# Graph network on one core: node tiles below 52 split in row form and turned by DMA in the node update

## The reference, cut to what matters

```python
u = mish(jnp.concatenate([x, agg], axis=-1) @ W3 + b3)
out = u @ W4 + b4
y = x + out
mu = jnp.mean(y, axis=-1, keepdims=True)
var = jnp.mean(jnp.square(y - mu), axis=-1, keepdims=True)
return (y - mu) * jax.lax.rsqrt(var + LN_EPS) * gamma + beta
...
x = x + _L2_gnn_ref(h, ...)
h = jnp.maximum(_layernorm(x, axis=-1), 0.0)
x = x + _L3_gnn_ref(h, ...)
```

## Time and profile before

| | us |
|---|---|
| median of 3 runs | 2869.98 (2865.81 to 2870.67) |
| the profiled execution's own time | 2869.94 |
| its span, first to last instruction | 2867.5 |
| node update, first W3 matmul to its last VectorE instruction | 1900.3 to 2448.8 |
| PE busy over the span | 2449.1 (85%) |
| DVE busy | 1900.3 (66%) |
| ACT busy | 1508.1 (53%) |
| POOL busy | 1197.0 (42%) |

### The profile page before, as it was taken

One profiled execution on the slowest core, in us unless ns is written; L12 is line 12 of the kernel. 1 busy time (PEld: TensorE's weight loads), 2 busy tenths in 40 slices (PEclk: granted clock), 3 DMA queues, 4 the chain that ended last, 5 costly groups with the idle time before them and its releaser, 6 DMA issues. The chain is left out here.

```text
span 2867.5 us, 45056 instructions
## 1 busy us (share of the span) xinstructions
PE 2449.1 (85%) x13348; PEld 1420.4 (50%) x13348; DVE 1900.3 (66%) x4585; ACT 1508.1 (53%) x2234; POOL 1197.0 (42%) x1984
## 2 busy tenths in 40 slices
PE   0437998799879999899996988989999998899965
PEld 0424554344444445444553546766666665344443
DVE  7634887678657876799874445658888888323344
ACT  5524675445334543355434775658888777232261
POOL 5656775336333332355554531114444444001146
PEclk9998999999999999999998999999999999999975
DMA  8443453278757888766654332223333344101268
GB/s 200 166 154 111 149 151 104 101 189 203 140 116 186 208 179 153 204 221 221 202 183 141 103 105 74 83 94 126 117 124 117 132 148 136 57 1 42 60 233 343
DMA packets 379310, 414.16 MB, mean 144 GB/s; under 512 B 198240, under 2 KB 237573, under 8 KB 376206
## 3 DMA queue, kind: packets, MB, share of 16 engines
q1 hardware_dynamic: 350510, 337.43, 40.1%
q0 software_dynamic: 28640, 74.78, 9.0%
HBM read 172.55 MB, written 198.32 MB: 129 GB/s over the span
## 5 line engine op out<-in xcount | busy, mean ns | idle before, releaser
L218 PE MATMUL s_ps_z<-s_w,slots 128*128 128x512 f16 x2844 | 640.0, 383 | 7.9 <-DMA s_w<-split_self 7.9
L218 PEld LDWEIGHTS s_ps_z<-s_w,slots 128*128 128x128 f16 (+1 forms) x2844 | 279.5, 99 | 325.2 <-issue 10.7
L1649 ACT ACTIVATE s_g<-s_g,s_rn 128x512 f32<-128x512 f32 x237 | 169.8, 716 | 226.8 <-POOL s_rn L1508 226.7
L1508 POOL TENSOR_TENSOR s_rn<-s_em,minus_half 128x1 f32<-128x1 f32 x237 | 178.6, 754 | 219.6 <-DVE s_em L1577 214.5
L1558 DVE SCALAR_TENSOR_TENSOR s_g<-s_ps_z,s_f,s_bias 128x512 f32<-128x512 f32 x237 | 177.9, 751 | 109.6 <-PE s_ps_z L218 96.4
L2459 PE MATMUL u_ps_z<-slots,weights 128*128 (+2 forms) x1920 | 215.2, 273 | 4.1 <-PEq L166 4.1
L2595 PE MATMUL z_ps_z<-slots,weights 128*128 128x512 f16 (+1 forms) x960 | 211.8, 381 | 3.0 <-PEq L166 3.0
L2459 PEld LDWEIGHTS u_ps_z<-slots,weights 128*128 128x128 f16 x1920 | 186.4, 98 | 26.3 <-issue 4.3
L2564 DVE BATCH_NORM_STATS2 z_stats<-slots 128x6 f32<-128x512 f32 (+1 forms) x76 | 52.2, 687 | 187.2 <-ACT slots L2581 187.2
L1568 DVE SCALAR_TENSOR_TENSOR s_junk<-s_g 128x512 f32<-128x512 f32 x237 | 164.5, 694 | 4.1
L218 PE MATMUL s_ps_z<-s_wn,s_aT 128*128 128x512 f16 x720 | 165.2, 380 | 1.8 <-DVE s_aT L1392 1.8
(11 more groups left out here) (395 smaller groups left out, 5615.0 us busy)
## 6 DMA issues: line engine op xcount, KB each, us to landing
h_rows<-s_g SPq DMA_DIRECT2D x237, 256.0 KB, 2.4
x_rows<-q_x SPq DMA_DIRECT2D x79, 256.0 KB, 2.3
s_halves<-x_rows SPq DMA_DIRECT2D x79, 256.0 KB, 2.9
x_rows<-s_halves SPq DMA_DIRECT2D x79, 256.0 KB, 2.1
u_x<-x_rows SPq DMA_DIRECT2D x79, 256.0 KB, 2.9
x_rows<-u_x SPq DMA_DIRECT2D x79, 256.0 KB, 2.1
h_rows<-u_h SPq DMA_DIRECT2D x79, 256.0 KB
weights<-x_rows SPq DMA_DIRECT2D x79, 256.0 KB, 6.6
```

The lines of the kernel that those rows point to most:

```text
L218: ins = nc.tensor.matmul(out_ap, a(c), w[:, part * size + c * n:part * size + (c + 1) * n], start=first and c == 0 and m == 0, stop=stop a ...
L1508: nc.gpsimd.tensor_tensor(out=self.rn[b][:, :], in0=self.em[b][:, :], in1=minus_half[:, :], op=POW).then_inc(self.s_rn, 1)
L1649: nc.scalar.activation(self.g[b][:, :], self.g[b][:, :], ACT.Relu, scale=self.rn[v.buf(2)][:, 0:1]).then_inc(self.s_h, 1)
```

## The change

For tiles 0 to 51 (`PE_TURNS = 52`; steps 2 to 27 handle them) TensorE no longer transposes. ScalarE's `hi` reads the rows `u_h` and writes their high half in row form into the `u_zg` buffer, VectorE's `lo` writes the low half beside it, and SyncE turns both with one DMA per tile into `slots`. Tiles 52 to 78 are turned by TensorE as before. For all tiles `hi` moves ahead of `hi_u` on ScalarE, and `lo` moves from behind `centred` and `add_messages` to behind `times_z`, ahead of `lo_u`, on VectorE. The loads of `u_x` stand at the head of SyncE's step in both kernels.

```diff
+    PAIR_LOOP_END = 28
...
+    PE_TURNS = 2 * (PAIR_LOOP_END - 2)
+    assert PE_TURNS < FT - 1
+
+    def pe_turns(v):
+        return isinstance(v.t, int) and v.t >= PE_TURNS
...
+            rows16 = [t[:, :].bitcast(F16) for t in zg]
...
+                        else:
+                            sp.wait_ge(turn_out[e], 16 * (PE_TURNS // 2))
                         sp.dma_start(zg[e % 2][:, :], zagg_d[:, e * D:(e + 1) * D]).then_inc(zg_in[e % 2], 16)
...
+                def turn(v):
+                    if not pe_turns(v):
+                        b = v.buf(2)
+                        sp.wait_ge(s_lo, v.t + 1)
+                        sp.dma_start_transpose(
+                            slots16[:, bass.ds(v.t * 2 * D, 2 * D)].rearrange("p (c n) -> p c n", n=P),
+                            rows16[b]).then_inc(turn_out[b], 16)
...
                     of_pair(v, 2, store_h)
+                    of_pair(v, 2, turn)
...
                 def lo(v):
+                    b = v.buf(2)
                     dve.wait_ge(s_hi, v.t + 1)
...
+                    else:
+                        nc.vector.scalar_tensor_tensor(out=rows16[b][:, D:2 * D], in0=h4[b][:, :], scalar=SCALE_LN,
+                                                       in1=rows16[b][:, 0:D], op0=MUL, op1=SUB).then_inc(s_lo, 1)
...
                     whole_pair(v, 0, times_z)
+                    of_pair(v, 2, lo)
                     whole_pair(v, 0, lo_u(0))
...
                     of_pair(v, -1, add_messages(1))
-                    of_pair(v, 2, lo)
                     of_pair(v, 1, residual, (1,))
...
+                    if pe_turns(v.later(-2)):
+                        act.wait_ge(s_turn, v.t - 1 - PE_TURNS)
+                    else:
+                        wait_count(act, s_lo, v.t - 1)
                     wait_count(act, h_out[b], 16 * v.uses(2))
...
+                    else:
+                        act.wait_ge(s_h4, v.t + 1)
+                        wait_count(act, turn_out[b], 16 * v.uses(2))
+                        nc.scalar.activation(rows16[b][:, 0:D], h4[b][:, :], ACT.Copy, scale=SCALE_LN).then_inc(s_hi, 1)
...
                     of_pair(v, 2, next_rows, (1,))
+                    of_pair(v, 2, hi)
                     whole_pair(v, 0, hi_u)
-                    of_pair(v, 2, hi)
...
                 def turn(v):
+                    if pe_turns(v):
+                        pe.wait_ge(s_h4, v.t + 1)
+                        wait_count(pe, s_lo, v.t - 1)
+                        transposes(pe, ps_t[v.buf(2)], h4[v.buf(2)]).then_inc(s_turn, 1)
```

More of the change, by code:

```diff
@@ L2100, in _ @@
                 pipeline(pe, ET, (0, message), (2, project), (1, sums), peel=ET, loop_end=ET)
+    PAIR_LOOP_END = 28
     def by_pairs(eng, step):
-        groups, peel, loop_end = (NT + 1) // 2, 6, 28
+        groups, peel, loop_end = (NT + 1) // 2, 6, PAIR_LOOP_END
         for g in range(peel):
@@ L2156, in node_update @@
             x_in, x_out, h_out = pair("u", "xin", 4), pair("u", "xout", 4), pair("u", "hout")
[L2157 removed]
+            zg_in, turn_out = pair("u", "zgin"), pair("u", "turnout")
             normy, norm3 = Norm(ctx, "u_ny", 2), Norm(ctx, "u_n3", 2)
@@ L2367, in lo @@
                 def lo(v):
+                    b = v.buf(2)
                     dve.wait_ge(s_hi, v.t + 1)
-                    nc.vector.scalar_tensor_tensor(out=slot_lo(v.t), in0=ps_t[v.buf(2)][:, :], scalar=SCALE_LN,
-                                                   in1=slot_hi(v.t), op0=MUL, op1=SUB).then_inc(s_lo, 1)
+                    if pe_turns(v):
+                        nc.vector.scalar_tensor_tensor(out=slot_lo(v.t), in0=ps_t[b][:, :], scalar=SCALE_LN,
+                                                       in1=slot_hi(v.t), op0=MUL, op1=SUB).then_inc(s_lo, 1)
+                    else:
+                        nc.vector.scalar_tensor_tensor(out=rows16[b][:, D:2 * D], in0=h4[b][:, :], scalar=SCALE_LN,
+                                                       in1=rows16[b][:, 0:D], op0=MUL, op1=SUB).then_inc(s_lo, 1)
                 def step(v):
@@ L2430, in hi @@
                 def hi(v):
-                    act.wait_ge(s_turn, v.t + 1)
-                    nc.scalar.activation(slot_hi(v.t), ps_t[v.buf(2)][:, :], ACT.Copy,
-                                         scale=SCALE_LN).then_inc(s_hi, 1)
+                    b = v.buf(2)
+                    if pe_turns(v):
+                        act.wait_ge(s_turn, v.t + 1 - PE_TURNS)
+                        nc.scalar.activation(slot_hi(v.t), ps_t[b][:, :], ACT.Copy, scale=SCALE_LN).then_inc(s_hi, 1)
+                    else:
+                        act.wait_ge(s_h4, v.t + 1)
+                        wait_count(act, turn_out[b], 16 * v.uses(2))
+                        nc.scalar.activation(rows16[b][:, 0:D], h4[b][:, :], ACT.Copy, scale=SCALE_LN).then_inc(s_hi, 1)
                 def step(v):
@@ L2492, in turn @@
                 def turn(v):
-                    pe.wait_ge(s_h4, v.t + 1)
-                    wait_count(pe, s_lo, v.t - 1)
-                    transposes(pe, ps_t[v.buf(2)], h4[v.buf(2)]).then_inc(s_turn, 1)
+                    if pe_turns(v):
+                        pe.wait_ge(s_h4, v.t + 1)
+                        wait_count(pe, s_lo, v.t - 1)
+                        transposes(pe, ps_t[v.buf(2)], h4[v.buf(2)]).then_inc(s_turn, 1)
                 def step(v):
```

1 line of the change is left out of this document (removed).

## The result

The changed kernel takes **2904.72 us** (median of 4 runs, 2900.78 to 2905.93). The kernel before, timed beside it, takes 2870.32 (4 runs, 2865.81 to 2874.16). The ratio is 1.0125, interval 1.0112 to 1.0139: slower, by 34.4 us, where 37 had been forecast. The profiled execution took 2905.87 us, 35.9 more than that of before, and its span is 2904.2.

A forecast was written before the change was run, and what follows sets the result against it. A ring over ScalarE, VectorE and GpSimd (12.70 us) was taken to lie just behind TensorE's 13.03 us and to set the zone's pace. 2869.94 + 20.8 (steps 2 to 27) + 16.2 (28 to 39) = 2906.9, forecast 2907 us, range 2890 to 2925.

The forecast's parts named there:

- the ring of 12.70 us: Steps before the zone: a once-a-step chain of waits over ScalarE, VectorE and GpSimd, 12.70 us against the step's 13.03.
- The change's timetable: Steps 2 to 27: start times with `hi` and `lo` ahead of `hi_u` and `lo_u`; ring grows 1.13 us, step 0.80.
- Zone, +1.35 a step: Steps 28 to 39, TensorE still transposing: second `hi` waits for a transpose, ring grows about 1.35 us, +16.2 us in all.
- TensorE's saving is worth nothing: Steps 2 to 27: TensorE loses 0.87 us a step, but the ring's 13.83 us sets the step, so nothing is gained.
- the busy share that the forecast named: Sign to look for in steps 6 to 27: TensorE busy 88% instead of 100%.
- SyncE and DMA, nothing: Each step adds two transposes of 1.24 us issue on SyncE; later loads of `u_x` and DMA traffic cost nothing.
- the cover of 4: SyncE: the 4 us by which loads of `u_x` may slip before ScalarE or GpSimd would wait.
- the rival at 3085 us: DMA transposes at the skill page's single-block price: 21 us a step, 208 us over, about 3085 us; chance 0.01.
- TensorE's clock: Rival: waits of about 1.7 us a step lower TensorE's clock, step 14.2 us, about 2920 us in all; chance 0.06.
- the freed TensorE decides: Rival: ring grows by less than 0.33 us, so the kernel gets faster, 2861 or 2847 us; chance 0.08.
- a draw: Rival: ring grows by about 0.3 us in both parts and the ends cancel, near 2870 us; chance 0.04.
- Transposes that come late: Rival: tiles take over 6 us to land or `u_x` loads slip over 4 us, say 2930 us; chance 0.01.

The follow-up runs named there:

- e3: Changed kernel with `hi` behind `hi_u`, `lo` between first `residual` and second `centred`, transposes one step later, tiles from 52 on in the old order; ratio 1.0036.
- e9: Kernel before, TensorE transposing every tile, with only the first tile's `next_rows` moved behind `tanh` in steps 0 to 27; ratio 1.0053.
- e6: e5 with `hi` behind `hi_u`, `lo` behind the second `centred`, and the transposes issued one step later; ratio 0.9943.
- e5: Changed kernel with tiles from 52 on in the old order and the first tile's `next_rows` behind `tanh` in steps below 28; ratio 0.9969.
- e10: e6 with the first tile's `next_rows` behind `tanh` in the steps from 28 on too; 2843.82 us, ratio 0.9916.
- e7: Changed kernel with TensorE also transposing the tiles below 52, into banks that nobody reads; ratio 1.0131.
- e4: Changed kernel with a second DMA transpose of each row-form tile, into the slot of the tile two before; ratio 1.0109.
- e8: Changed kernel with tiles from 52 on in the old order and, below 52, `lo` at its old place behind the second `centred`; ratio 1.0157.
- e11: Kernel before with `lo` moved between the first `residual` and the second `centred`, reading one operand from PSUM; ratio 1.0045.

## Why the prediction was right, step by step

- **Windows and the ring of 12.70 us** (slack 0.33): right, to 0.1 us. The loop's changed step (13.78 in the mean) less the growth of 1.11 us below is 12.67, and e3's 13.46 less its 0.82 us on GpSimd is 12.64. The kernel before shows the ring by itself once: from the `hi_u` of step 1 to that of step 2, where TensorE sits idle for 1.50 us, it takes 12.61 us, and only 11.38 in e9, whose ring is cut. e6, and two written-out steps of e5, go below the ring too. One thing the forecast didn't know: where the ring sets the pace, a step in the hardware loop is longer than a written-out one (13.74 and 13.82 against 13.65, in e3 13.44 and 13.52 against 13.35). Where TensorE sets it, in the kernel before, both take 13.03. The reason is open.
- **The change's timetable.** Forecast from `next_rows` on: `hi` +0.70, `lo` +1.38, `hi_u` +1.78, `lo_u` +2.59, `residual` +3.99. Measured: +0.71, +1.35, +1.75, +2.56, +3.89. Without the change and without TensorE, `residual` stands at 2290.74 - 2287.96 = +2.78 (the zone rows of before above), where the forecast had +2.86. So the ring grew by 1.11 us, for 1.13. The pair of `lo_u` was read 0.07 too long (1.40 us to `residual`, measured 1.33), but on both sides, so it drops out of the growth. Row-form `hi` took 0.52 from start to start (two last 1.13), near the 0.54 chosen. Ring and growth together are 13.78 for 13.83, hence 0.755 a step instead of 0.80, and 19.3 us instead of 20.8.
- **Zone, +1.35 a step.** The growth was right to 0.01 us, its cause too (the second `hi` behind a transpose). One sentence was wrong: "the same ring, made longer by `add_messages`". e10 and the zone rows of before shown there say that this ring closes through `add_messages` and `sigmoid`, not through `u_n_sh` and `next_rows`. The number stands because both rings share the stretch from `next_rows` to `residual`, which is what grew. The twelve steps came to 16.8 us, for 16.2.
- **TensorE's saving is worth nothing; it will stand idle 1.7 us a step.** The first half is shown by e7. The second half is true of its work (12.16 of 13.8), but the busy share that the forecast named, 88%, reads 94%: the rows of L2512 last 0.3 us longer than before, twice a step, and TensorE's waits add up to 0.9 us a step. The sign to look for was the wrong one; the waits by line are the better one.
- **SyncE and DMA, nothing.** The transposes were issued at 2116.14 in 2.65 us, took 3.1 to 3.3 us to land, and the loads of `u_x` went out 5.40 us behind the second `next_rows` instead of 1.43. The forecast had 4.67; they slipped by 3.97 us, just within the cover of 4, and nothing waits for them. The DMA share is 53% against a bound of 62%. e4 shows that even 73% is free.
- **The price of a single block.** The DMA issues of the stretch say that eight blocks land in 3.2 us (median of 40), so the rival at 3085 us fell; by the Trainium skill, "VectorE: DVE Perf Modes", "The three transpose paths", they would take an estimated 10.5 one after another, and the trace disagrees. (The rival's own sum is off: 2870 + 208 + 16 is 3094.)

```profile
slots<-u_zg SPq DMA_TRANSPOSE x40, 3.2
```

- **TensorE's clock.** Up to 2293 us, past the `hi_u` of step 27 (2281.0), the granted clock stayed at 1.00, as forecast. Behind that it did not quite: 0.97 in the window above. The windows of 1 us behind a wait of TensorE of 2.00 us, up to 2293.79, show it:

```profile
2292.00:2293.00 1.00, 0.00 (x0) 0.00 (x0) 0.45 (x2) 1.00 (x3) 1.00 (x2) 1.00 0.00 0
...
2294.00:2295.00 1.00, 1.00 (x6) 0.88 (x6) 0.90 (x2) 0.29 (x2) 0.00 (x0) 0.50 0.40 145
...
2298.00:2299.00 1.00, 1.00 (x11) 0.89 (x10) 0.94 (x2) 0.00 (x0) 0.00 (x0) 1.00 0.00 0
```

For some 3 us the clock is at its lower level, and 48 matmuls of `update` take 6.66 instead of 5.40 us. In four places up to 2424 us this happens (not behind every long wait: none followed that of 2.54 us up to 2373.12); three zone steps, the ones that contain such a fall, are longer than 15.80 (16.01, 15.84, 16.26), 0.7 us in all. The rival was real and small. That it stayed small because TensorE isn't the bound there is argued, not tested.

The other rivals: "the freed TensorE decides" failed at its own condition, growth under 0.33 us (it was 1.11), and a draw likewise. Transposes that come late didn't appear in any kernel here.

## What to carry to other kernels

An engine that is busy 100% of a stretch may have a ring of other engines (a chain of waits that closes once a step) a third of a microsecond behind it; work it out before taking work off the busy engine, and above all before putting the replaced work on that ring. Cutting such a ring (here one `next_rows` moved behind `tanh`) and relieving the busy engine may each lose alone and win together: 1.0053, 1.0125, and 0.9943 for both with the old order (0.9916 with the cut in all steps). When an instruction changes which buffer it reads, look for whose wait it ends: `lo` now frees `u_h`, which is why its late place, the right one in the kernel before, cost 0.9 us a step in e8.

## What the hardware showed that was not expected

GpSimd and VectorE get in each other's way when VectorE reads two operands from the on-chip memory SBUF. GpSimd's operations on one column go from 0.19 to 0.55 and 0.65 us beside the row form of `lo` (e3), and stay at 0.19 beside the form that reads PSUM (e11). In the other direction two `lo` of 1.28 us last 2.38 beside GpSimd's `add_beta` (e5). Each time one side alone paid: `lo` kept its length in e3 (two in 1.26 us), `add_beta` kept its 2.50 us in e5. The Trainium skill, "Advanced Engine Details and Errata", "GPSIMD Details", names this conflict for VectorE instructions with two SBUF inputs; e3 and e11 agree, and the prices are these. The prediction allowed 0.10 us an instruction for it, and nothing for GpSimd's side.

A DMA transpose of a whole tile in this stage cost the compute engines nothing that could be measured, at 53% and 73% DMA share where the ring set the step, and at 61% where TensorE did (e6).
